# A macaron layer on one core: three stages put into one program block, attention's opening work placed beside the first feed-forward stage and its closing turn split around the opening of the second

## The chip, the cores and the metric

The kernel runs on one core of one Trainium2 chip. The number reported is device time in microseconds (us). The run of the kernel before has a median of 1843.06 us over three executions (1840.89 to 1844.34). One of them, at 1844.34 us, was also recorded by the hardware profiler; every row of a trace below is of that execution. A core has a matmul engine (PE, TensorE), a vector engine (DVE), an activation engine (ACT), a general engine (POOL, GpSimd) and SP, which here only issues DMAs. Each runs its own instructions in program order and waits for the others on semaphores.

## The reference

x has 32 sequences of 256 tokens of width 128, so 8192 rows. Three sublayers follow each other, each on the layer-normalised result of the one before:

```python
x = x + 0.5 * ffn(layernorm(x))     # mixture of experts
x = x + attention(layernorm(x))     # causal, differential, 16 heads of width 8
x = x + 0.5 * ffn(layernorm(x))     # the same weights as the first

# ffn: 8 experts of width 256, two of them picked by a sigmoid gate for each token
comb = zeros(T, 8); comb[top2] = top2_scores / (sum + 1e-6)
h    = silu(einsum('td,ehd->teh', xf, w1))
out  = einsum('te,ted->td', comb, einsum('teh,edh->ted', h, w2))

# attention: two softmaxes over rotated queries and keys, subtracted
attn = softmax(q1 k1) - lam[head] * softmax(q2 k2)
out  = rmsnorm(attn @ v) * head_norm_w * (1 - LAMBDA_INIT);  out @ Wo.T + bo
```

## The kernel before, in words

`build` calls `ffn` (ffn1), `attention`, `ffn` (ffn2). Each of the three opens an `nc.Block()` of its own with one program per engine. Where one block ends and the next begins, all engines meet, and SP first waits until its stores have landed (`sp.wait_ge(stored, ...)`).

**A feed-forward stage** works on 16 blocks of 512 tokens. `blocks` calls `body(Block(c))` on every engine for c = -2 to 16. In the body of block c, PE makes the products of block c, while block c+2 is loaded, normalised and transposed ("read") and block c+1 goes through its gate ("gated"). Inside a body there are eight steps e, one for each expert: PE makes the up product of expert e (L567) into one of two PSUM buffers and the down product of expert e-3 (L580); ACT applies silu (L334) and rounds h to its high part (L341); DVE scales by the gate (`scale`, L479); the low part is made by POOL for experts 0 to 5 (L292) and by DVE for 6 and 7 (L487). The up product of expert e+2 waits for `scale` of expert e, because it writes the same PSUM buffer. The gate runs as: logits on PE (L547), two small DVE operations (L402, L405), two `pow` instructions on POOL (`gate_exp`, L284), thirteen short rounds on DVE that end in `comb` (L470), a transposition (L557), a copy to rows (L328). In the bodies c = -2 and -1 nothing overlaps with products, so there this chain runs bare: the first up product stands in PE's order behind the logits of block 1, and these wait for the rows of block 0. In body -1 POOL runs `gate_exp(0)`, `ln_rstd(1)`, `gate_exp(1)` (the halves of block 0's gate with the reciprocal root of block 1 between them), and DVE runs `mean_shift`, then the gate rounds, with `weight_low(2)` (L499, the low part of w2) in the middle of them at e = 4.

**Attention** works on 32 sequences. `turns` calls `body(Turn(i))` for i = -1 to 34. A turn walks through `ORDER`, a list written by hand of units such as XT (transposition of the normalised x), QK and V (projections), S (scores by query, read by DVE for row maxima), T (scores by key, read by ACT as exp), NT, OT and OP (the end of a sequence); `offset` says which sequence each unit serves in a turn, and `AFTER` says behind which unit the other engines' work stands. Ahead of the turns stands a set-up: SP loads x of sequence 0 and thirteen tensors in all, POOL makes masks, clears `qs` (L997) and `v` (L1000, L1002) and then raises `v_set`; DVE takes statistics of sequence 0, clears `kd` (L1204), makes the low part of the weights (L1211), `biased` in two passes (L1215, L1221) and waits for `v_set` before its first turn. ACT splits `wqk`, then waits for all nine small loads, splits `wv` (L1097), and only then copies the first transposition (L1040). PE's first projection waits for DVE's `xt_low` (L1190). The last turn, 34, holds only the end of sequence 31: ms (DVE L1182, L1185), `rms` (POOL `pow`, L978), `scaled` (POOL L983 to L993), OT, the ACT copy (L1064), OP, the addition (DVE L1178) and the store.

## Time and profile before

| | us |
|---|---|
| median of three runs | 1843.06 |
| the profiled execution | 1844.34 |
| its span, first to last instruction | 1842.6 |
| ffn1: opening, to the first up product | 0 to 32.2 |
| ffn1: products, to the last addition | 32.2 to 433.3 |
| between the last addition and attention's first projection | 433.3 to 450.6 |
| attention's turns, to the last `ms_eps` | 450.6 to 1394.9 |
| from there to ffn2's first up product | 1394.9 to 1439.0 |
| ffn2: products, to the end | 1439.0 to 1842.6 |

PE is busy for 1615.4 us, 88% of the span; DVE 73%, POOL 72%, ACT 65%. By stage PE is busy for 395.8 of 401.1 us in ffn1's products and 395.4 of 403.6 in ffn2's, for 754.3 of 854.9 in attention from 540 to 1394.9, and for 0.7 of 17.3, and 8.6 of 44.1, in the two stretches between the stages. A row of the timeline reads: start, duration, engine, line, operation, tile written <- tiles read, shape, count, and in square brackets how long the engine sat idle before it and what ended that. SPq rows are DMA issues.

### The profile page before, as it was taken

Reading aid. Unit: us, or ns where it says so; the run is one execution under the profiler, and the core shown is the slowest. Engines: PE = TensorE matmul, PEld = TensorE weight load, DVE = VectorE, ACT = ScalarE, POOL = GpSimd, SP = SyncE. Lnnn points to the kernel's source line nnn. Section 1 sums busy time; section 2 is a strip of 40 time slices with the busy share of each in tenths; the row PEclk is TensorE's granted clock in tenths of the full one; section 3 lists DMA queues with packets and bytes.
Section 4 is the critical chain, followed back from the end, with each engine's and each line's share of the span. In section 5 each row is a group of like instructions: output and inputs, shape, how many; then the busy total and the mean of one; then the engine's idle time right before and its main releaser. Section 6 shows DMA issues by size and latency. Waiting matters only on the chain. (4 is left out here: it accounts for less than half of the span.)

```text
span 1842.6 us, 43587 instructions
## 1 busy us (share of the span) xinstructions
PE 1615.4 (88%) x16768; PEld 1235.1 (67%) x16768; DVE 1343.6 (73%) x3034; ACT 1199.4 (65%) x1581; POOL 1319.9 (72%) x836
## 2 busy tenths in 40 slices
PE   4999999995478998988989888998872799999998
PEld 3787778784356666666666666666651688778787
DVE  5777777765678788888878788788732677777775
ACT  4777777772156676666666576676662577777776
POOL 4888888875447677767767677677634688888885
PEclk9999999997589999999999999999996899999999
DMA  3333233332222332332232322332302233233331
GB/s 115 104 116 111 86 104 116 104 104 53 78 67 74 94 89 63 93 92 71 83 88 69 88 83 70 92 87 65 88 17 71 99 115 114 82 105 115 104 110 63
DMA packets 143678, 163.16 MB, mean 89 GB/s; under 512 B 13244, under 2 KB 125582, under 8 KB 142478
## 3 DMA queue, kind: packets, MB, share of 16 engines
q1 hardware_dynamic: 143472, 160.38, 28.5%
q8 instruction: 133, 2.18, 0.5%
q14 instruction: 73, 0.60, 0.1%
HBM read 91.20 MB, written 14.70 MB: 57 GB/s over the span
## 5 line engine op out<-in xcount | busy, mean ns | idle before, releaser
L292 POOL TENSOR_TENSOR ffn_h_low<-ffn_h,ffn_h_high 128x1024 fp32r<-128x1024 f32 x192 | 458.8, 2403 | 94.8 <-ACT ffn_h_high L341 94.8
L1046 ACT ACTIVATE att_prob<-att_ring 128x1024 f32<-128x1024 f32 x384 | 390.3, 1024 | 181.4 <-PE att_ring L1280 180.7
L1159 DVE TENSOR_REDUCE att_nmax<-att_ring 128x4 f32<-128x1024 f32 (+1 forms) x384 | 453.2, 1215 | 39.8 <-PE att_ring L1280 36.8
L479 DVE TENSOR_TENSOR ffn_h<-ffn_up,ffn_comb_wide 128x1024 f32<-128x1024 f32 x256 | 311.1, 1215 | 125.9 <-ACT ffn_up L334 125.7
L334 ACT ACTIVATE ffn_up<-ffn_up 128x1024 f32<-128x1024 f32 x256 | 258.1, 1008 | 201.9 <-PE ffn_up L567 200.2
L341 ACT ACTIVATE ffn_h_high<-ffn_h 128x1024 fp32r<-128x1024 f32 x256 | 269.3, 1052 | 0.7 <-DVE ffn_h L479 0.7
L978 POOL TENSOR_TENSOR att_rrms<-att_ms_eps,att_minus_halves 128x32 f32<-128x32 f32 x32 | 174.1, 5440 | 67.6 <-DVE att_ms_eps L1185 67.6
L1280 PE MATMUL att_ring<-att_qs,att_kd 64*128 64x256 bf16 (+1 forms) x2048 | 153.2, 249 | 76.9 <-DVE att_nmax L1159 24.9
L567 PE MATMUL ffn_up<-ffn_xt_high,ffn_w_high 128*128 128x512 f32 x512 | 214.8, 419 | 1.6 <-DVE ffn_h L479 1.5
L284 POOL TENSOR_TENSOR ffn_ez<-ffn_e_const,ffn_nz 128x16 f32<-128x16 f32 x64 | 185.7, 2903 | 38.8 <-DVE ffn_nz L405 38.8
L580 PE MATMUL ffn_y<-ffn_h_high,ffn_w_high 128*128 128x512 f32 x512 | 205.4, 401 | 6.4 <-POOL ffn_h_low L292 5.0
L1295 PE MATMUL att_o_ps<-att_prob,att_v 128*32 128x256 f32 (+1 forms) x4096 | 201.5, 339 | 5.5 <-ACT att_prob L1046 5.5
L567 PE MATMUL ffn_up<-ffn_xt_low,ffn_w_high 128*128 128x512 f32 x512 | 203.6, 398 | 0.0
L567 PE MATMUL ffn_up<-ffn_xt_high,ffn_w_low 128*128 128x512 f32 x512 | 203.4, 397 | 0.0
L580 PE MATMUL ffn_y<-ffn_h_low,ffn_w_high 128*128 128x512 f32 x512 | 201.4, 393 | 0.0
L580 PE MATMUL ffn_y<-ffn_h_high,ffn_w_low 128*128 128x512 f32 x512 | 200.0, 391 | 0.0
L1280 PE MATMUL att_ring<-att_kd,att_qs 64*128 64x256 bf16 (+1 forms) x2048 | 153.3, 249 | 37.5 <-DVE att_nmax L1159 21.7
L1295 PEld LDWEIGHTS att_o_ps<-att_prob,att_v 128*32 128x32 f32 x4096 | 118.0, 113 | 70.0 <-issue 11.8
L1280 PEld LDWEIGHTS att_ring<-att_qs,att_kd 64*128 64x128 bf16 x2048 | 63.0, 95 | 135.6 <-DVE att_nmax L1159 61.1
L960 POOL TENSOR_TENSOR att_parts<-att_left,att_parts 128x512 bf16<-128x512 f32 x64 | 74.2, 1159 | 100.7 <-ACT att_parts L1057 100.7
L1280 PEld LDWEIGHTS att_ring<-att_kd,att_qs 64*128 64x128 bf16 x2048 | 69.9, 95 | 86.5 <-DVE att_nmax L1159 43.4
L580 PEld LDWEIGHTS ffn_y<-ffn_h_high,ffn_w_high 128*128 128x128 f32 x512 | 96.0, 188 | 42.4 <-POOL ffn_h_low L292 19.2
(152 smaller groups left out, 3248.8 us busy)
## 6 DMA issues: line engine op xcount, KB each, us to landing
ffn_comb_wide<-ffn_comb_d SPq DMA_DIRECT2D x128, 512.0 KB, 5.7
att_qs<-att_parts SPq DMA_DIRECT2D x192, 128.0 KB, 2.4
att_kd<-att_parts SPq DMA_DIRECT2D x192, 128.0 KB, 2.4
ffn_x<-x SPq DMA_DIRECT2D x32, 256.0 KB, 3.1
ffn_w<-w SPq DMA_DIRECT2D x4, 1024.0 KB, 7.6
x<-ffn_out SPq DMA_DIRECT2D x16, 256.0 KB, 2.4
att_x<-x SPq DMA_DIRECT2D x32, 128.0 KB, 2.3
att_xr<-x SPq DMA_DIRECT2D x32, 128.0 KB, 2.3
```

Source lines behind the costliest of these rows:

```text
L284: nc.gpsimd.tensor_tensor(ez[:, k].rearrange("p t e -> p (t e)"), e_const[:, 0:n], nz[:, k].rearrange("p t e -> p (t e)"), ALU.pow).then_i ...
L292: nc.gpsimd.tensor_tensor(hts[1][:, e % NH], h[:, e % NH], hts[0][:, e % NH], ALU.subtract).then_inc(low_by_pool, 1)
L334: nc.scalar.activation(up[:, e % NUP], up[:, e % NUP], ACT.Silu).then_inc(silu_ready, 1)
L341: nc.scalar.activation(hts[0][:, e % NH], h[:, e % NH], ACT.Copy).then_inc(high_ready, 1)
L479: nc.vector.tensor_tensor(h[:, e % NH], up[:, e % NUP], comb_wide[:, b.c % NW, e].unsqueeze(1).to_broadcast([P, HE, FT]), ALU.mult).then_i ...
L567: last = nc.tensor.matmul(up[:, e % NUP, k], w1s[a1][:, col:col + P], xts[a2][:, b.slot()], start=(n == 0), stop=(n == 2))
L580: last = nc.tensor.matmul(y[:], w2s[a1][:, col:col + D], hts[a2][:, e % NH, k], start=(e == 0 and k == 0 and n == 0), stop=(e == E - 1 and ...
L978: nc.gpsimd.tensor_tensor(rrms[:], ms_eps[:], minus_halves[:], ALU.pow).then_inc(rrms_ready, 1)
L1046: nc.scalar.activation(prob[:, u % NP], ring[:, ORDER.index((kind, u)) % 3], ACT.Exp, scale=SCALE).then_inc(prob_ready, 1)
L1159: nc.vector.tensor_reduce(nmax[:, b, :, h0:h0 + cnt], ring[:, pos % 3] .rearrange("p (s h k) -> p s h k", s=2, k=width), AX.X, ALU.max, ne ...
L1280: return nc.tensor.matmul(out, lhs, rhs, start=start, stop=stop)
L1295: last = nc.tensor.matmul(o_ps[VW * i:VW * (i + 1), g % 2, j, b * P:S], v[:, k, b, h], p, start=(b == 0), stop=(b == 1), tile_position=(0, ...
```

## The change

One function, `layer`, replaces `attention` and opens a single block for all three stages. `ffn` no longer runs anything: it returns for each engine a triple of set-up, body and end. The engines' programs are strung together without a meeting point; the joints are waits on counters that exist already. `finished` waits for ffn1's last addition. `gone` (six waits on each engine) is what ffn2's set-up waits for, `banks_free` stands ahead of ffn2's first up product. Tiles of attention that are needed early (`front`) lie where ffn1's raw weights lay, which is why `split_done` stands ahead of their loads; ffn2's tiles lie over attention's except those of the closing turn (`tail`).

Beside ffn1's blocks run now: POOL's masks (ahead of body -1), DVE's `ones_set` (ahead of body 0), SP's mask DMAs (ahead of body 3), the thirteen loads (ahead of body 12), ACT's `split` and DVE's `early` (ahead of body 14), DVE's `late` and POOL's `ln_rstd` (ahead of body 15), DVE's `mean_shift` (ahead of body 16). `kd`, `qs` and `v` are cleared as before, behind `finished`. In both feed-forward stages, in body -1, `ln_rstd(1)` comes behind both halves of `gate_exp(0)`, `mean_shift` behind the gate's first rounds, and `weight_low(2)` at e = 6, behind the gate. The output tile has two slots in place of four, and three PSUM banks change places. At the end of attention `ORDER` of turn 34 is cut: its first unit (with ms and rms) runs, then ffn2's set-up and body -2, then the rest of the turn, then body -1. The first DMA of that cut turn (xr) goes ahead of ffn2's loads and its store behind body -2. The diff, cut to its core:

```diff
+                if e == 1 and read.exists() and b.c != -1:
+                    ln_rstd(read)
+                if e in (0, 1) and gated.exists():
+                    gate_exp(gated, e)
+                if e == 1 and b.c == -1:
+                    ln_rstd(read)
...
+                if e == 6 and b.c == -1:
+                    weight_low(2)
...
+def blocks_beside(program, **beside):
+
+    setup, body, _ = program
+    setup()
     for c in range(-2, FB + 1):
+        if f"before_{c + 2}" in beside:
+            beside[f"before_{c + 2}"]()
         body(Block(c))
...
+def turns(body, first, following):
+
+    setup, ffn_body, end = following
+    for i in range(first, B + 2):
+        body(Turn(i))
+    body(Turn(B + 2), OPENING)
+    setup()
+    ffn_body(Block(-2))
+    body(Turn(B + 2), CLOSING)
+    for c in range(-1, FB + 1):
+        ffn_body(Block(c))
+    if end:
+        end()
...
+        def gone(engine):
+
+            engine.wait_ge(pv_done, 4 * B)
+            engine.wait_ge(prob_ready, 12 * B)
+            engine.wait_ge(pe["T"], 12 * B)
+            engine.wait_ge(o_copied, 4 * B)
+            engine.wait_ge(max_in, 32 * B)
+            engine.wait_ge(left_step, 4 * B)
...
+                blocks_beside(ffn1_sync(sp), before_5=masks, before_14=loads)
+                sp.wait_ge(ones_out, 16)
+                sp.wait_ge(masks_in, 16 * 4)
+                finished(sp)
+                turns(body, -1, ffn_sync(sp))
...
+                blocks_beside(ffn1_gpsimd(pool), before_1=constants, before_17=lambda: ln_rstd(Turn(-2)))
+                finished(pool)
                 clear_queries(0)
...
+                def split():
+                    split_done(act)
+                    act.wait_ge(wqk_in, 16)
+                    nc.scalar.activation(wqks[0][:], wqk[:], ACT.Copy).then_inc(weight_high, 1)
+                    act.wait_ge(weights_in, 16 * 9)
+                    nc.scalar.activation(wvs[0][:], wv[:], ACT.Copy).then_inc(weight_high, 1)
+
+                blocks_beside(ffn1_scalar(act), before_16=split)
+                normalise(Turn(-2))
+                finished(act)
...
+                def early():
+                    split_done(dve)
+                    ln_stats(first)
+                    dve.wait_ge(rope_in, 32)
+                    for u in range(2):
+                        for c in range(2):
+                            last = nc.vector.tensor_scalar(biased[:, u, c], rope[:, 0], bqk[:, 4 * u + c:4 * u + c + 1], None,
+                                                           ALU.mult)
+                    last.then_inc(bias_step, 1)
+
+                def late():
+                    dve.wait_ge(bias_step, 1)
+                    for u in range(2):
+                        for c in range(2):
+                            last = nc.vector.scalar_tensor_tensor(out=biased[:, u, c], in0=rope[:, 1],
+                                                                  scalar=bqk[:, 4 * u + 2 + c:4 * u + 3 + c], in1=biased[:, u, c],
+                                                                  op0=ALU.mult, op1=ALU.add)
+                    last.then_inc(bias_step, 1)
+                    dve.wait_ge(weight_high, 2)
+                    nc.vector.tensor_tensor(wqks[1][:], wqk[:], wqks[0][:], ALU.subtract).then_inc(weight_low, 1)
+                    nc.vector.tensor_tensor(wvs[1][:], wv[:], wvs[0][:], ALU.subtract).then_inc(weight_low, 1)
+
+                blocks_beside(ffn1_vector(dve), before_2=ones_set, before_16=early, before_17=late,
+                              before_18=lambda: mean_shift(first))
+                finished(dve)
```

(The index in `before_17` counts from body -2, so it stands ahead of body 15.)

## Rows read from the trace of the kernel before

**Rows 1.** DVE's timeline in ffn1's opening.

```profile
20.71 0.20 DVE L443 TENSOR_SCALAR ffn_scratch<-ffn_ez 128x32 f32<-128x32 f32 x1 [2.78 <-POOL ffn_ez L284]
...
25.33 2.28 DVE L499 TENSOR_TENSOR ffn_w_low<-ffn_w,ffn_w_high 128x2048 fp32r<-128x2048 f32 x1
...
28.45 0.19 DVE L470 TENSOR_TENSOR ffn_comb<-ffn_scratch,ffn_rdenom 128x32 f32<-128x32 f32 x1
```

**Rows 2.** POOL's timeline in ffn1's opening.

```profile
16.15 1.58 POOL L277 TENSOR_TENSOR ffn_rstd<-ffn_var_eps,ffn_minus_half 128x4 f32<-128x4 f32 x1
```

**Rows 3.** Timelines of DVE, POOL, ACT and PE between ffn1 and attention.

```profile
432.65 0.69 DVE L494 TENSOR_TENSOR ffn_out<-ffn_turn_ps,ffn_x 128x512 f32<-128x512 f32 x1 [3.25 <-PE ffn_turn_ps L591]
...
442.82 1.80 POOL L997 MEMSET att_qs<- 128x2048 uint32 x1
...
447.27 0.30 POOL L1002 MEMSET att_v<- 128x96 f32 x1
...
447.94 0.31 ACT L1097 ACTIVATE att_wv_high<-att_wv 128x128 fp32r<-128x128 f32 x1 [5.80 <-DMA att_lam_in<-lk]
...
450.62 0.55 PE L1280 MATMUL att_ring<-att_xt_high,att_wqk_high 128*128 128x256 f32 x1 [5.92 <-DVE att_xt_low L1190]
```

**Rows 4.** Timelines of DVE, POOL and PE at the turn from body 14 to 15.

```profile
403.02 1.23 DVE L479 TENSOR_TENSOR ffn_h<-ffn_up,ffn_comb_wide 128x1024 f32<-128x1024 f32 x1 [1.56 <-ACT ffn_up L334]
...
401.25 2.41 POOL L292 TENSOR_TENSOR ffn_h_low<-ffn_h,ffn_h_high 128x1024 fp32r<-128x1024 f32 x1 [0.82 <-ACT ffn_h_high L341]
...
405.94 0.40 PE L567 MATMUL ffn_up<-ffn_xt_high,ffn_w_high 128*128 128x512 f32 x1
```

**Rows 5.** DVE's set-up of attention: low weights and both passes of `biased`.

```profile
442.35 1.59 DVE L1211 TENSOR_TENSOR att_wqk_low<-att_wqk,att_wqk_high 128x1024 fp32r<-128x1024 f32 x1
443.87 4.37 DVE L1215 TENSOR_SCALAR att_biased<-att_rope,att_bqk 128x256 f32<-128x256 f32 x4
448.27 1.67 DVE L1221 SCALAR_TENSOR_TENSOR att_biased<-att_rope,att_bqk,att_biased 128x256 f32<-128x256 f32 x4
```

**Rows 6.** DVE and POOL operations side by side, attention's first turn, then body 14.

```profile
465.73 1.11 DVE L1123 SCALAR_TENSOR_TENSOR att_shift<-att_mean_var,att_rstd 128x2 f32<-128x2 f32 x1 [7.44 <-POOL att_rstd L919]
...
465.67 1.16 POOL L960 TENSOR_TENSOR att_parts<-att_left,att_parts 128x512 bf16<-128x512 f32 x1
...
379.50 5.77 POOL L284 TENSOR_TENSOR ffn_ez<-ffn_e_const,ffn_nz 128x16 f32<-128x16 f32 x2
...
380.95 1.21 DVE L487 TENSOR_TENSOR ffn_h_low<-ffn_h,ffn_h_high 128x1024 fp32r<-128x1024 f32 x1
```

**Rows 7.** PE's timeline at a late landing; its window: length, five engines' busy time, clock, DMA share.

```profile
925.43 0.61 PE L1280 MATMUL att_ring<-att_qs,att_kd 64*128 64x256 bf16 x4 [2.46 <-DMA att_qs<-att_max_rows]
...
925.00:930.00 5.00, 4.57 (x56) 3.02 (x56) 1.50 (x3) 2.43 (x3) 0.89 (x2) 0.50 0.52 145
```

**Rows 8.** Timelines of SP, POOL, ACT and DVE between attention and ffn2.

```profile
1394.96 0.42 SPq L868 DMA_DIRECT2D att_xr<-x  x1
...
1407.32 0.36 SPq L221 DMA_DIRECT2D ffn_x<-x  x1
...
1394.99 5.44 POOL L978 TENSOR_TENSOR att_rrms<-att_ms_eps,att_minus_halves 128x32 f32<-128x32 f32 x1 [1.32 <-DVE att_ms_eps L1185]
...
1402.78 0.38 ACT L1064 ACTIVATE att_of_t<-att_ring 128x256 f32<-128x256 f32 x1 [9.70 <-PE att_ring L1360]
...
1413.64 1.63 ACT L316 ACTIVATE ffn_xn<-ffn_x,ffn_shift,ffn_rstd 128x128 f32<-128x128 f32 x4
...
1418.61 3.71 ACT L309 ACTIVATE ffn_w_high<-ffn_w 128x2048 fp32r<-128x2048 f32 x2 [1.48 <-DMA ffn_w<-w]
...
1404.54 0.42 DVE L1178 TENSOR_TENSOR att_xo<-att_ring,att_xrb 128x256 f32<-128x256 f32 x1 [9.63 <-PE att_ring L1280]
...
1420.11 0.19 DVE L405 SCALAR_TENSOR_TENSOR ffn_nz<-ffn_gate_ps,ffn_z_low 128x32 f32<-128x32 f32 x1
...
1435.26 0.19 DVE L470 TENSOR_TENSOR ffn_comb<-ffn_scratch,ffn_rdenom 128x32 f32<-128x32 f32 x1
```

More of the change, by code:

```diff
@@ L732, in attention @@
[L732 to L741 removed]
+        wo = sb("wo", [P, D], to=tail)
@@ new lines, in layer, with raw_weights @@
+        hide_t = sb("hide_t", [P, 4, TILE], BF16, to=tail)
+        halves = sb("halves", [4, 2, S], BF16, to=tail)
+        one_rows = sb("one_rows", [16, 3 * H * S // 16], BF16, to=tail)
+        minus_half = sb("minus_half", [P, QB], to=tail)
+        def raw_weights(to, name):
+            return [to.enter_context(nc.sbuf_tensor(f"{name}_{n}", [P, E * EH], F32)) for n in ("w1", "w2")]
+        raw1 = raw_weights(raw, tag1)
+        raw.close()
+        wqk = sb("wqk", [P, 2 * NC4, P], to=front)
@@ new lines, in layer @@
+        var_eps = sb("var_eps", [P, QB], to=front)
+        rstd = sb("rstd", [P, QB], to=front)
+        shift = sb("shift", [P, QB], to=front)
+        xn = sb("xn", [P, QB, D], to=front)
+        wqks = [sb(f"wqk_{n}", [P, 2 * NC4, P], F32R, to=front) for n in ("high", "low")]
+        wvs = [sb(f"wv_{n}", [P, D], F32R, to=front) for n in ("high", "low")]
+        biased = sb("biased", [P, 2, 2, S], to=front)
+        stage1, (split_done, finished, rows_stored) = ffn(nc, tag1, x_first, x_in, w, *raw1, first_stage, ctx)
@@ L820, in wait_unit, with banks_free, stored_for @@
             wait(engine, pe[kind], turn.at(offset(kind, n), UNITS[kind], n + 1))
+        rest.close()
+        front.close()
+        def gone(engine):
[5 more added lines that the diff above has]
+            engine.wait_ge(left_step, 4 * B)
+        def banks_free(engine):
+            engine.wait_ge(read["OT"], B)
+            engine.wait_ge(read["OP"], B)
+        def stored_for(engine, b):
+            engine.wait_ge(stored, 16 * min(B, FT // S * (b.c + 1)))
+        after = After(sync=gone, gpsimd=gone, scalar=gone, vector=gone, tensor=gone, up=banks_free, stored=stored_for)
+        stage2, _ = ffn(nc, tag2, x_mid, x_out2, w, *raw_weights(ctx, tag2), ctx, ctx, after)
+        ffn_sync, ffn_gpsimd, ffn_scalar, ffn_vector, ffn_tensor = stage2
         with nc.Block() as block:
@@ L860, in set_rows, with body @@
                                      ).then_inc(rows_in[k], 16)
-                def body(turn):
+                def body(turn, part=WHOLE):
                     if turn.runs(2):
                         load_x(turn)
-                    if turn.runs(-3):
+                    if turn.runs(-3) and part is not CLOSING:
                         wait_apart(sp, read["OP"], turn.at(-4, 1, 1))
@@ L1028, in _, with body @@
                 pool.wait_ge(lam_step, 5)
-                turns(body, 0)
+                turns(body, 0, ffn_gpsimd(pool))
             @block.scalar
             def _(act):
-                def body(turn):
-                    for kind, u in ORDER:
+                def body(turn, part=WHOLE):
+                    for kind, u in ORDER[part]:
                         if kind == "XT" and turn.runs(1):
@@ L1211, in _ @@
-                nc.vector.tensor_tensor(wqks[1][:], wqk[:], wqks[0][:], ALU.subtract).then_inc(weight_low, 1)
-                dve.wait_ge(rope_in, 32)
-                for u in range(2):
-                    for c in range(2):
-                        last = nc.vector.tensor_scalar(biased[:, u, c], rope[:, 0], bqk[:, 4 * u + c:4 * u + c + 1], None,
-                                                       ALU.mult)
-                last.then_inc(bias_step, 1)
-                dve.wait_ge(bias_step, 1)
@@ L1423, in build @@
     x2 = nc.dram_tensor("x2", (T, D), F32).ap()
-    ffn(nc, "ffn1", a["x"], x1, a)
-    attention(nc, "att", x1, x2, a)
-    ffn(nc, "ffn2", x2, out, a)
+    layer(nc, a["x"], "ffn1", x1, "att", x2, "ffn2", out, a)
 def kernel(**inputs):
```

1106 lines of the change are left out of this document (552 added, 554 removed).

## The prediction

> **What bounds the kernel now.** I read the page's shares first and then the engines' busy time by stage (both are in the section on the profile). Inside the products of both feed-forward stages PE is busy for 98 to 99% of the time, so there only what makes PE wait counts. In the 17.3 us between ffn1 and attention it is busy for 0.7, in the 44.1 between the last ms_eps and ffn2's first up product for 8.6. In these stretches, and in ffn1's opening, every engine mostly waits for another, so there I read each engine's timeline row by row and looked for what ended last. Attention itself keeps its order of work; its PE losses there are mostly waits for a DMA's landing, which the change doesn't touch. The sum has four terms.
>
> **Term 1, ffn1's opening: -3.6.** The gate's rounds start on DVE at 20.71, as soon as POOL's second gate_exp half is there [rows 1]. Between the halves POOL made rstd of block 1, 1.58 us [rows 2]. Behind both halves it frees 1.58: the gate starts at 19.1. weight_low(2), 2.28 at 25.33, stands inside the rounds; it now follows comb [rows 1]. mean_shift needs rstd(1), now only ready about 1.0 after the second half (the 1.58 held some waiting), so it ends some 0.2 later than its turn. Comb was done at 28.45 + 0.19 = 28.64; now 28.64 - 1.58 - 2.28 + 0.22 = 25.0. Transposition, comb_rows, logits of block 1 and the first up product follow at an unchanged distance. weight_low(2) runs from 25 to 27.3, ahead of the first up product at 28.6. Ends: -3.0, if mean_shift costs 0.8, and -3.6.
>
> **Term 2, attention's work beside ffn1's blocks: +3.0** (0 to +7). Here the change adds instructions ahead of work that PE waits for. What costs nothing: POOL's constants fall where POOL idles before the first gate input comes, SP's 4 masks and 13 loads stand on a queue with nothing urgent but a block's x (asked for two blocks ahead), DVE's ones_set in an idle gap of body 0, ACT's splits (0.31 for the 128 columns of wv [rows 3], about 1.0 for wqk) in its idle time; if their cover were gone, they would cost their own 1 to 6 us once. DVE is what matters, as up(e+2) waits for scale(e). At the turn to body 15 DVE waits 1.56 and does scale at 403.02; PE starts the up product behind it at 405.94, 1.7 us after scale's end at 404.25 [rows 4]. So a scale may be 1.7 late for nothing. late adds 1.67 (four fused passes), 1.59 (wqk_low) [rows 5] and 0.3 (wv_low): 3.55, starting at 401.5. Unhindered it ends at 405.0, scale is 2.0 late, which is close to free. But DVE operations with two SBUF inputs seem to be held while POOL streams: a 128x2 operation that started at 465.73 took 1.11, until POOL's at 465.67 + 1.16 was over [rows 6]. POOL's h_low of 2.41 starts at 401.25 [rows 4] and lasts to 403.66. Thus the first pass is held to there, and late ends at 403.7 + 1.4 + 1.2 + 0.3 + gaps = 406.9 (the 1.67 and 1.59 hold little waits of their own). Scale ends at 408.1, and up(15,1), which stood at 405.94, starts at 408.1: a stall of 2.2. early's tensor_scalars show 4.37 [rows 5], but they start 442.35 + 1.59 to 448.27, beside POOL's clears from 442.82 on [rows 3]; unheld I take about 1.0 for four, ending 1.0 behind their slot, inside the slack of 1.7: nothing. (All 4.37 unhidden would be 2.7 over the slack, which is in the upper end.) mean_shift ahead of body 16 is held until h_low's end: 2.41 after its start, where scale stood at 403.02 - 401.25 = 1.77 [rows 4], so 0.64 + 0.2 = +0.8 in a body that ends the stage. 2.2 + 0.8 = 3.0. The lower end: no holding.
>
> **Term 3, ffn1 to attention: -11.7** (-10.5 to -13). Before: the last addition ends at 432.65 + 0.69 = 433.34. Then come the meeting of the engines, the loads (ACT waited 5.80 for lam_in and split wv until 448.25), xt_low, and the first projection at 450.62 [rows 3]: 17.3. Also in it: POOL's clears, 442.82 to 447.27 + 0.30 = 447.57, so 4.75 [rows 3]. After: loads, splits, statistics, biased and the normalised x of sequence 0 are ready; only POOL's clears remain behind finished, with kd's on DVE, which is shorter. v_set comes at 433.34 + 0.1 + 4.75 = 438.2. DVE waits for it ahead of its first turn, so xt_low (0.4) and the projection come at 438.9. 450.62 - 438.9 = 11.7. What is late next is POOL, alone. PE idles 5.6 in it; after an idle of only 2.46 its clock was granted at 0.50, 1.2 GHz [rows 7], so I assume that level here as before, and no gain. Were it to stay at 2.4 GHz, -1.3 more. The upper end is set-up work of some 1.2 us (SP's set_rows, ACT's copy) that falls behind v_set.
>
> **Term 4, attention's end and ffn2's opening: -13.5** (-9 to -13.5). The anchor is rrms on POOL, 1394.99 + 5.44 = 1400.43; the closing turn's xr load goes out at 1394.96, and x of block 0 now right behind it, at about 1396 in place of 1407.32 [rows 8]. Behind rrms POOL clears small constants and makes rstd(0): together 2.1 (with rstd at 1.58 [rows 2], 2.5). xn of block 0 starts at 1402.55, not 1413.64; nz, which ended at 1420.11 + 0.19 = 1420.30, ends at 1409.2 [rows 8]: 11.1 earlier. ACT's w_high needs 3.71 and had waited for w [rows 8]; the first weights are asked for 11 earlier too, so it ends near 1410.1. Only then come ACT's of_t, OP, and the addition xo: before, from of_t at 1402.78 to xo's end at 1404.96, 2.2 [rows 8]; now the end is 1412.2. So attention's last store, no longer on the path, hides behind the opening. gate_exp(0) on POOL, both halves, 5.77 as in body 14 [rows 6], ends at 1415.0. DVE, behind xo, has statistics of block 1 (about 1.5) and weight_low(1) (2.28 by [rows 1]), to 1416.1: DVE is now late, by 1. The gate's rounds, from 20.71 to 28.64 less the 2.28 [rows 1], are 5.65, with mean_shift 5.8: comb at 1421.95, not 1435.26 + 0.19 = 1435.45 [rows 8]. -13.5. The lower gain: weights land 4.5 later, because x, xr and w share the queues.
>
> **The sum** is -3.6 + 3.0 - 11.7 - 13.5 = -25.8. The profiled execution, 1844.34 (span 1842.6, 1.7 around it), becomes 1818.5, its span 1816.8; it was 1.28 above the median, so the median becomes 1843.06 - 25.8 = **1817.3**.
>
> **The rivals.** **B, cover is complete**: DVE's two-input operations aren't held by POOL, term 2 is 0, and 1814.3. For it: L487 (two SBUF inputs) at 380.95 took 1.21 beside a POOL pow [rows 6]. Against it: 465.73 in the same group, beside a streaming POOL. **C, pow holds as well**: early's operations stand beside gate_exp of body 14, 379.50 to 385.27 [rows 6]. If any POOL instruction held DVE until it ends, they would finish near 386.5, and the scales behind be 5.5 late, less 1.7: +3.8, 1821.1. The row at 380.95 speaks against it. The Trainium skill (SBUF — State Buffer, section "SBUF: two separate sides") has the pair shared by DVE and GpSimd as an exclusive lock "for the whole instruction", for DVE operations in a two-port mode or with two SBUF inputs; taken literally that is rival C, and the trace agrees for the streaming POOL operations only. **D, boundary 2 is worth less**: w lands late or ACT, which takes w_high ahead of of_t, delays xo and with it DVE's statistics: 4.5 less, 1821.8. For it: w had kept ACT waiting 1.48 even behind the engines' meeting [rows 8]. **E, the joints don't overlap**: the joints' waits end so late that only the meetings go and the openings' new order stays. From xo's end, 1404.96, to x's issue at 1407.32 a meeting cost 2.36 [rows 8]; twice that and twice 3.6 make 11.9: 1831.1. Against it: every counter in gone is of turns before the last. **F, slower**: attention's chain from max_rows to qs gets later, since the counters and tiles now carry over from ffn1. PE waited 2.46 for that DMA at 925.43 and ran 5 us at 1.2 GHz in place of 2.4 [rows 7]: 2.46 + 5 x 0.5 = 5.0 for such a turn. From 6 more such turns on (30 us) the gain is gone; in 28 turns it would be +140 - 26, so 1957. Against it: order, buffers and DMAs within the turns stay the same.
>
> **How the numbers follow.** Forecast 58%, B 12%, C 10%, D 12%, E 4%, F 4%. The range takes in forecast, B, C and D with the ends of the terms: low 1811.5 (term 2 at 0, term 3 at -13, with half of what term 4 may yet give), high 1826.0 (C and D together give 1825.6). E and F stay out. A measurement can tell 0.2%, 3.7 us, about the spread of the three runs. Every case but F is faster by more: faster 0.94; 0.02 for F stopping near six turns; slower 0.04.
>
> **What would show it.** Term 1: DVE's first gate rounds at 19.1, comb near 25.0, first up near 28.6. Term 2: up(15,1) waits about 2.2 for scale, late's first pass starts or ends at POOL's h_low's end, and no wait in bodies 12 to 14; if late's rows show their bare durations, B. Term 3: first projection 5.6 after the last addition, released by xt_low behind v_set, POOL without a gap. Term 4: x of block 0 issued within 2 us of xr, xn about 2 behind rrms, xo between bodies -2 and -1, first up 30.6 after the last ms_eps, where 44.1 stood. The prediction is wrong if attention's turns take longer, if ACT's w_high ends much after 1410 on this scale, or if PE starts ffn2 with a stall at a weight.

## The result: 1843.7 to 1815.85 us

Over four executions each, the median went from 1843.7 us (1840.89 to 1845.09) to 1815.85 (1811.61 to 1820.04), a ratio of 0.985 with a 95% interval of 0.982 to 0.988. That is 27.9 us less; forecast were 25.8 less and 1817.3. The profiled execution took 1812.79, its span is 1811.0, against 1844.34 and 1842.6 before: 31.6 less. Its six stretches (start of the first up product; to the end of the last addition; to the first projection; to the last ms_eps; to ffn2's first up product; to the end) show where they went. A joint is the stretch between two stages; the second is counted from the start of the last ms_eps, 0.2 ahead of its end, from which the 44.1 and 30.6 of the prediction count.

| stretch | before | changed | difference | forecast |
|---|---|---|---|---|
| ffn1, opening | 32.17 | 29.38 | -2.79 | -3.6 |
| ffn1, products | 401.17 | 403.39 | +2.22 | +3.0 |
| first joint | 17.28 | 5.45 | -11.83 | -11.7 |
| attention | 944.11 | 938.17 | -5.94 | 0 |
| second joint and ffn2's opening | 44.25 | 30.96 | -13.29 | -13.5 |
| ffn2, products | 403.62 | 403.65 | +0.03 | 0 |

The four stretches that have a forecast term changed by -25.69 together, where -25.8 stood. The rest of the profiled difference is attention, whose turns the change leaves alone.

In every timeline row below, the columns are start, duration, engine, line, operation, tile written <- tiles read, shape, count, and in brackets the idle time before it and what ended it. First PE at the landmarks of the changed kernel, the first projection among them, which answers to the last row of [rows 3]:

```profile
29.38 0.77 PE L574 MATMUL ffn_up<-ffn_xt_high,ffn_w_high 128*128 128x512 f32 x1
...
404.75 0.50 PE L574 MATMUL ffn_up<-ffn_xt_high,ffn_w_high 128*128 128x512 f32 x1 [1.54 <-DVE ffn_h L485]
...
438.22 0.55 PE L1398 MATMUL att_ring<-att_xt_high,att_wqk_high 128*128 128x256 f32 x1 [4.93 <-DVE att_xt_low L1295]
...
1407.35 0.77 PE L574 MATMUL ffn_up<-ffn_xt_high,ffn_w_high 128*128 128x512 f32 x1
```

**The opening of ffn1**, POOL and then DVE, against [rows 1, 2]:

```profile
13.23 6.33 POOL L282 TENSOR_TENSOR ffn_ez<-ffn_e_const,ffn_nz 128x16 f32<-128x16 f32 x2 [2.03 <-DVE ffn_nz L411]
19.54 1.00 POOL L275 TENSOR_TENSOR ffn_rstd<-ffn_var_eps,ffn_minus_half 128x4 f32<-128x4 f32 x1
```

```profile
14.53 2.28 DVE L505 TENSOR_TENSOR ffn_w_low<-ffn_w,ffn_w_high 128x2048 fp32r<-128x2048 f32 x1
19.68 0.20 DVE L449 TENSOR_SCALAR ffn_scratch<-ffn_ez 128x32 f32<-128x32 f32 x1 [2.86 <-POOL ffn_ez L282]
...
25.64 0.19 DVE L476 TENSOR_TENSOR ffn_comb<-ffn_scratch,ffn_rdenom 128x32 f32<-128x32 f32 x1
```

rstd now takes 1.00 where it took 1.58 in the middle [rows 2]. The 0.58 didn't vanish: the pair of pow instructions takes 6.33, and two such took 5.77 in [rows 6]. POOL was waiting in its second instruction until DVE's weight_low, 14.53 + 2.28 = 16.81, was over, and whichever instruction stands second bears that.

**The price beside the blocks**, DVE and POOL at bodies 15 and 16, against [rows 4]:

```profile
398.48 3.74 DVE L1327 SCALAR_TENSOR_TENSOR att_biased<-att_rope,att_bqk,att_biased 128x256 f32<-128x256 f32 x4
402.14 1.21 DVE L1332 TENSOR_TENSOR att_wqk_low<-att_wqk,att_wqk_high 128x1024 fp32r<-128x1024 f32 x1
...
423.05 2.27 DVE L1228 SCALAR_TENSOR_TENSOR att_shift<-att_mean_var,att_rstd 128x2 f32<-128x2 f32 x1
```

```profile
398.35 2.40 POOL L290 TENSOR_TENSOR ffn_h_low<-ffn_h,ffn_h_high 128x1024 fp32r<-128x1024 f32 x1 [0.82 <-ACT ffn_h_high L344]
...
422.92 2.39 POOL L290 TENSOR_TENSOR ffn_h_low<-ffn_h,ffn_h_high 128x1024 fp32r<-128x1024 f32 x1 [0.36 <-ACT ffn_h_high L344]
```

The first fused pass begins as POOL streams h_low (to 400.75), and the four take 3.74 in place of 1.67 [rows 5]. mean_shift, on 128x2 elements, takes 2.27, to POOL's 425.31.

**The first joint**: POOL's three clears run from 432.83 to 437.56, DVE's xt_low stands right behind them, and nothing else is late:

```profile
432.83 1.81 POOL L1097 MEMSET att_qs<- 128x2048 uint32 x1 [7.53 <-DVE ffn_out L500]
434.57 2.66 POOL L1102 MEMSET att_v<- 128x3072 f32 x1
437.30 0.26 POOL L1104 MEMSET att_v<- 128x96 f32 x1
```

```profile
433.27 1.76 DVE L1340 MEMSET att_kd<- 128x2048 uint32 x1 [0.49 <-DVE ffn_out L500]
437.64 0.43 DVE L1295 TENSOR_TENSOR att_xt_low<-att_ring,att_xt_high 128x256 fp32r<-128x256 f32 x1 [2.61 <-POOL att_v L1104]
```

**The second joint**, SP, POOL, ACT and DVE, against [rows 8]. The last ms_eps starts at 1376.39:

```profile
1377.28 0.36 SPq L212 DMA_DIRECT2D ffn_x<-x  x1
...
1376.65 5.44 POOL L1078 TENSOR_TENSOR att_rrms<-att_ms_eps,att_minus_halves 128x32 f32<-128x32 f32 x1 [1.32 <-DVE att_ms_eps L1290]
...
1382.84 1.02 POOL L275 TENSOR_TENSOR ffn_rstd<-ffn_var_eps,ffn_minus_half 128x4 f32<-128x4 f32 x1
...
1396.59 2.22 POOL L275 TENSOR_TENSOR ffn_rstd<-ffn_var_eps,ffn_minus_half 128x4 f32<-128x4 f32 x1
...
1384.09 1.65 ACT L319 ACTIVATE ffn_xn<-ffn_x,ffn_shift,ffn_rstd 128x128 f32<-128x128 f32 x4 [1.96 <-DVE ffn_shift L396]
...
1388.50 3.71 ACT L312 ACTIVATE ffn_w_high<-ffn_w 128x2048 fp32r<-128x2048 f32 x2 [0.90 <-DMA ffn_w<-w]
1392.12 0.36 ACT L1166 ACTIVATE att_of_t<-att_ring 128x256 f32<-128x256 f32 x1
...
1393.86 0.42 DVE L1283 TENSOR_TENSOR att_xo<-att_ring,att_xrb 128x256 f32<-128x256 f32 x1 [3.08 <-PE att_ring L1398]
...
1395.66 2.28 DVE L505 TENSOR_TENSOR ffn_w_low<-ffn_w,ffn_w_high 128x2048 fp32r<-128x2048 f32 x1
1397.86 0.19 DVE L449 TENSOR_SCALAR ffn_scratch<-ffn_ez 128x32 f32<-128x32 f32 x1
```

x of block 0 is asked for 0.66 behind xr (1376.62), xn starts 2.0 behind rrms. ACT's w_high waited 0.90 for w, of_t stands behind it, xo behind of_t, weight_low(1) behind xo, and the gate's rounds start when that is over, at 1397.86, though both pow instructions were done at 1396.63.

### The profile page after: what moved, and what is told of

The parts are those of the page before. It is cut to its first block, busy times and chain, and to the rows that moved or that the text cites. A ratio compares the mean times of both kernels' runs of the same rounds, so it can differ in the third digit from the quotient of the medians.

```text
span 1811.0 us, 43617 instructions
## 1 busy us (share of the span) xinstructions
PE 1607.8 (89%) x16768; PEld 1229.6 (68%) x16768; DVE 1345.2 (74%) x3034; ACT 1198.5 (66%) x1581; POOL 1320.1 (73%) x836
## 3 DMA queue, kind: packets, MB, share of 16 engines
q1 hardware_dynamic: 143472, 160.38, 28.9%
## 4 chain that ended last, share of the span: by engine, by line
PE 44%; POOL 22%; issue 13%; DVE 11%; DMA 4%; ACT 4%; SPq 2%; POOLq 0%; DVEq 0%; ACTq 0%
PE att_ring L1398 13%; PE ffn_y L587 9%; PE ffn_up L574 9%; POOL ffn_ez L282 8%; PE att_o_ps L1413 7%; DVE att_nmax L1264 6%; POOL ffn_h_low L290 5%; POOL att_rrms L1078 3%; PE att_ring L1473 2%; POOL ffn_rstd L275 2%; DMA att_max_rows<-att_nmax_t 2%; ACT att_prob L1148 2%; ACT ffn_h_high L344 2%; DMA att_qs<-att_max_rows 2%; DVE att_turned L1243 1%
```

## Experiments

Executions of one kernel differ by several us, most of it in attention, so the experiments are read by the six stretches of their profiles, which repeat to within 0.1 to 0.5 where nothing was changed; the second joint adds to that up to 1.3, with w late by 0 to 1.2 on ACT, and attention varies by ten. Medians stand beside them. All edits are to the changed kernel.

| kernel | ffn1 opening | ffn1 products | joint 1 | attention | joint 2 | ffn2 | median |
|---|---|---|---|---|---|---|---|
| changed | 29.38 | 403.39 | 5.45 | 938.17 | 30.96 | 403.65 | 1815.85 |
| e1_order_undone | 32.29 | 403.53 | 5.45 | 944.17 | 35.57 | 403.79 | 1827.55 |
| e2_no_cover | 29.37 | 401.31 | 17.00 | 937.91 | 29.97 | 403.84 | 1821.81 |
| e3_turn_whole | 29.59 | 403.60 | 5.45 | 945.22 | 39.39 | 404.05 | 1831.66 |
| e4_v_wait_later | 29.56 | 403.45 | 2.68 | 937.83 | 30.00 | 403.78 | 1819.62 |
| e5_late_beside_pow | 29.43 | 405.81 | 5.45 | 939.02 | 29.95 | 403.84 | one run |
| e6_spread | 29.35 | 402.99 | 5.45 | 940.23 | 29.95 | 403.73 | one run |
| e7_low1_earlier | 30.94 | 403.63 | 5.45 | 938.09 | 31.73 | 403.86 | one run |
| e8_one_block_only | 29.41 | 401.24 | 15.60 | 948.48 | 31.28 | 403.69 | one run |
| e9_changed_again | 29.41 | 403.72 | 5.44 | 941.55 | 30.90 | 403.78 | 1820.0 |
| e10_best | 29.39 | 402.86 | 1.70 | 942.99 | 30.65 | 404.11 | 1817.07 |

e1 to e4 ran on one chip, beside 1846.83 for the kernel before; e9 and e10 on a second, beside 1848.86. e5 to e8 ran once each on a third (1815.23, 1813.44, 1815.47 and 1831.41, beside a single 1837.36), so they are read by their stretches alone.

### The order of body -1

```diff
-                if e == 1 and read.exists() and b.c != -1:
+                if e == 1 and read.exists():
                     ln_rstd(read)
                 if e in (0, 1) and gated.exists():
                     gate_exp(gated, e)
-                if e == 1 and b.c == -1:
-                    ln_rstd(read)
...
-                if e == 2 and read.exists() and b.c != -1:
+                if e == 2 and read.exists():
                     mean_shift(read)
...
-                if e == 2 and b.c == -1:
-                    mean_shift(read)
-                if e == 6 and b.c == -1:
+                if e == 4 and b.c == -1:
                     weight_low(2)
```

> The changed kernel, with body -1 of both feed-forward stages in the old order (rstd of block 1 between the two halves of the gate's exponential, mean_shift ahead of the gate's rounds, weight_low(2) inside them). Landmarks of the changed kernel's profile: first up product at 29.4 us, ffn1's products until the last addition 403.4, from there to the first projection 5.45, from the first projection to the last ms_eps 938.2, from there to ffn2's first up product 31.0, ffn2's products 403.6. My theory (the order counts in both openings, as DVE's gate rounds are the last chain in each): first up product at 32.2 (+2.8), and 33.9 in place of 31.0 at the second joint, +5.7 in all. Rival 1 (at the second joint DVE is late anyway because of the closing turn, so the order is worth nothing there): +2.8 in all. Rival 2 (the order counts for nothing, and ffn1's opening got shorter for another reason, such as an earlier landing): 0. All other stretches unchanged, except attention's, which may move by 6 either way.

The first opening got 2.9 longer, as expected. The second went to 35.57, and the kernels in which w landed in time show 29.95 to 30.00 there. Here w was in time too, so it got 5.6 longer, not 2.9. POOL and DVE of this kernel say why:

```profile
1399.90 2.91 POOL L282 TENSOR_TENSOR ffn_ez<-ffn_e_const,ffn_nz 128x16 f32<-128x16 f32 x1 [4.91 <-DVE ffn_nz L409]
1403.87 2.98 POOL L275 TENSOR_TENSOR ffn_rstd<-ffn_var_eps,ffn_minus_half 128x4 f32<-128x4 f32 x1 [1.06 <-DVE ffn_var_eps L388]
1406.83 2.89 POOL L282 TENSOR_TENSOR ffn_ez<-ffn_e_const,ffn_nz 128x16 f32<-128x16 f32 x1
```

```profile
1401.90 0.42 DVE L1279 TENSOR_TENSOR att_xo<-att_ring,att_xrb 128x256 f32<-128x256 f32 x1 [2.08 <-PE att_ring L1394]
...
1403.71 2.28 DVE L503 TENSOR_TENSOR ffn_w_low<-ffn_w,ffn_w_high 128x2048 fp32r<-128x2048 f32 x1
```

With the closing turn's addition ahead of it on DVE, var_eps of block 1 comes late, and rstd, standing between the two pow instructions, first waits 1.06 for it and then is held by weight_low until 1405.99. So the order and the split of the turn belong together: the split alone would have brought POOL a new wait in the middle of the gate.

### The overlap with ffn1's blocks

```diff
-                blocks_beside(ffn1_sync(sp), before_5=masks, before_14=loads)
+                blocks_beside(ffn1_sync(sp), before_5=masks)
+                loads()
...
-                blocks_beside(ffn1_gpsimd(pool), before_1=constants, before_17=lambda: ln_rstd(Turn(-2)))
+                blocks_beside(ffn1_gpsimd(pool), before_1=constants)
+                ln_rstd(Turn(-2))
...
-                blocks_beside(ffn1_scalar(act), before_16=split)
+                blocks_beside(ffn1_scalar(act))
+                split()
...
-                blocks_beside(ffn1_vector(dve), before_2=ones_set, before_16=early, before_17=late,
-                              before_18=lambda: mean_shift(first))
+                blocks_beside(ffn1_vector(dve), before_2=ones_set)
+                early()
+                late()
+                mean_shift(first)
```

> The changed kernel, with attention's thirteen loads, the splits, statistics, biased, rstd and mean_shift moved from beside ffn1's blocks to behind ffn1's last body; one block and no meeting of the engines, as in the changed kernel. My theory (it is the overlap that shortens the first joint, and the price beside the blocks is real): ffn1's products 401.2 in place of 403.4, and 14 (12.5 to 15.5) from the last addition to the first projection in place of 5.45, since the loads take some 9 to land and DVE's biased then meets POOL's clears again. Net +6.4. Rival 1 (the meeting of the engines was what cost): joint below 8, net about 0. Rival 2 (the meeting cost nothing): joint 17.3 as before the change, net +9.7.

ffn1's products fell to 401.31: the work beside the blocks costs 2.1. The joint took 17.00, not 14, near the 17.3 of rival 2 (the meeting cost nothing). But this order of the work is not that of the kernel before; the chain is another. Rows of DVE and ACT:

```profile
436.58 4.57 DVE L1322 TENSOR_SCALAR att_biased<-att_rope,att_bqk 128x256 f32<-128x256 f32 x4 [1.57 <-DMA att_bqk<-bqk]
```

```profile
442.94 0.31 ACT L1202 ACTIVATE att_wv_high<-att_wv 128x128 fp32r<-128x128 f32 x1 [6.13 <-DMA att_lam_in<-lk]
444.82 0.88 ACT L1187 ACTIVATE att_xn<-att_x,att_shift,att_rstd 128x128 f32<-128x128 f32 x2 [1.57 <-DVE att_shift L1231]
```

In this order mean_shift and xn stand behind everything of late, which the old order did not have, and late waits for the last small load. My 14 had left that out. So this run shows what the overlap covers in this order (11.5), not what the meeting cost. For that, the opening work went behind ffn1 in its old order, the constants and masks too:

```diff
-                blocks_beside(ffn1_sync(sp), before_5=masks, before_14=loads)
+                blocks_beside(ffn1_sync(sp))
+                loads()
+                masks()
...
-                blocks_beside(ffn1_vector(dve), before_2=ones_set, before_16=early, before_17=late,
-                              before_18=lambda: mean_shift(first))
+                blocks_beside(ffn1_vector(dve))
                 finished(dve)
+                ones_set()
+                ln_stats(first)
+                mean_shift(first)
```

> The changed kernel, with all of attention's opening work (constants, masks, loads, splits, statistics, biased, low parts) behind ffn1's last body, in the order in which the kernel before had it, so that at the first joint only the meeting of the engines and SP's final wait for its store are gone. In the kernel before SP issued the first load 2.8 after the last addition; here right behind the last store, some 0.6 after it. My theory (the meeting cost what it delayed the first load): 15.1 from the last addition to the first projection, in place of 17.3 before and 5.45 in the changed kernel, and ffn1's products 401.2. Rival 1 (the meeting cost nothing): 17.3. Rival 2 (it hid more, as engines could run ahead into their set-up): below 12.

15.60, by one execution, where 15.1 was expected: the meeting and SP's final wait were worth 1.7 of the 11.8 at this joint, the overlap the other 10.1, against 2.1 to 2.2 paid in the blocks.

### The split of the closing turn

```diff
-    body(Turn(B + 2), OPENING)
+    body(Turn(B + 2))
     setup()
     ffn_body(Block(-2))
-    body(Turn(B + 2), CLOSING)
```

> The changed kernel, with attention's last turn run as a whole ahead of ffn2's set-up and body -2. My theory (x of block 0 is then asked for behind the last store, 10 us later than 1377.3, and the opening hangs on it): ffn2's first up product 39.5 (38 to 41) behind the last ms_eps in place of 31.0, +8.5. Rival 1 (rrms on POOL, 5.4 us, sets the end, and what stands behind it in either order costs only its own 4.5): +4.5. Rival 2 (the split is worth nothing, w's landing sets the end): 0.

39.39, where 39.5 was expected. SP's queue shows what the opening hung on:

```profile
1394.23 0.36 SPq L992 DMA_DIRECT2D x<-att_xo  x1
1394.83 0.36 SPq L212 DMA_DIRECT2D ffn_x<-x  x1
```

The last ms_eps starts at 1383.86 there, so x is asked for 11.0 behind it, against 0.9 in the changed kernel. The split is worth 8.4 against the changed kernel's profile (9.4 against those with w in time). No run takes the second meeting out alone, but its price can be read: from xo's end, x is asked for 2.36 behind it in the kernel before (1404.96 to 1407.32, [rows 8]) and 0.74 behind it here (1394.09 to 1394.83). That is 1.6, and with the order at the first opening's 2.9 and the split's 8.4 it makes up nearly all of the 13.29.

### What holds a DVE operation beside POOL

```diff
-                blocks_beside(ffn1_vector(dve), before_2=ones_set, before_16=early, before_17=late,
+                blocks_beside(ffn1_vector(dve), before_2=ones_set, before_16=lambda: (early(), late()),
```

> The changed kernel, with DVE's late (four fused passes, wqk_low, wv_low) put directly behind early, ahead of body 14 in place of body 15. There POOL runs gate_exp's two pow instructions and not h_low. In the changed kernel the four passes took 3.74 us, until POOL's h_low ended, and the up product behind waited 1.54. My theory (a DVE operation with two SBUF inputs is held while POOL streams, and not while POOL computes a pow): the four passes take 1.2 to 1.7, wqk_low 1.2; in body 14 the scale behind them starts 3.1 later, of which 0.8 is slack, so PE waits about 2.3 there, and not at all in body 15; ffn1's products 404.1 in place of 403.4. Rival 1 (these passes are slow on their own): 3.7 here too, PE waits 4.5 in body 14, products 406.3. Rival 2 (any POOL instruction holds them until it ends, pow too): they end only with the second pow, near 382.8 on the changed kernel's scale, the scale behind is 6.6 late, PE waits 5.8.

DVE and POOL of this kernel:

```profile
378.21 1.68 DVE L1327 SCALAR_TENSOR_TENSOR att_biased<-att_rope,att_bqk,att_biased 128x256 f32<-128x256 f32 x4
```

```profile
377.01 6.97 POOL L282 TENSOR_TENSOR ffn_ez<-ffn_e_const,ffn_nz 128x16 f32<-128x16 f32 x2
```

The four passes take 1.68 beside pow and 3.74 beside h_low: rivals B and C of the prediction both fall, B since the holding is real, C since a pow that computes doesn't hold. PE waited 2.0 in body 14, near the 2.3 expected, and not in body 15. What I had wrong is the sum: 405.81, not 404.1. The difference is PE's clock. In these rows of PE a product takes 0.50 right behind the wait and 0.63 two us later:

```profile
382.41 0.50 PE L574 MATMUL ffn_up<-ffn_xt_high,ffn_w_high 128*128 128x512 f32 x1 [2.00 <-DVE ffn_h L485]
...
384.27 0.63 PE L587 MATMUL ffn_y<-ffn_h_high,ffn_w_high 128*128 128x512 f32 x1
```

From 384.4 to 386.8 the granted clock is 0.50, 1.2 GHz. The 24 products from 382.41 on take 7.23 us; behind the changed kernel's wait of 1.54 (at 404.75), where the clock stays at 1.00, 24 take 5.66. So the 0.46 more of waiting brought 1.57 of lost clock with it, which is nearly all of the 1.7 that I had missed.

The pow pair itself grew, from 5.77 in [rows 6] and 6.19 at the same place of the changed kernel to 6.97: its second instruction, which began beside wqk_low, took 4.10 in place of 2.90. The holding goes both ways, but here PE waited for none of it.

Of the other way, e7 was meant as an improvement and became the measurement:

```diff
-                if e == 0 and b.c == -1:
-                    weight_low(1)
...
                 if e == 7 and read.exists():
                     logits(read)
+                if e == 7 and b.c == -2:
+                    weight_low(1)
```

> The changed kernel, with DVE's weight_low(1) (2.28) at the end of body -2 in place of the start of body -1, in both feed-forward stages. In the changed kernel DVE stood idle for 3.1 before the closing turn's addition, and weight_low(1) behind it ended 1.2 after the gate's exponential was ready. My theory (DVE is the late one at the second joint, by that 1.2): from the last ms_eps to ffn2's first up product 28.8 to 29.8 in place of 31.0; in ffn1's opening POOL's second pow is no longer held by it, first up product at 28.9 in place of 29.4. Rival (ACT's copies, or w's landing, are the late ones): both unchanged, or later by up to 2.3 where weight_low waits for ACT ahead of the addition.

Both openings got longer, 1.5 and 1.8 (against 30.0), where both were expected to get shorter. The rival's number (later by up to 2.3) fits, but neither of its reasons is in the trace: w was in time, and the closing turn's addition came no later. DVE and POOL of the first opening are:

```profile
13.20 2.28 DVE L505 TENSOR_TENSOR ffn_w_low<-ffn_w,ffn_w_high 128x2048 fp32r<-128x2048 f32 x1
```

```profile
13.36 7.76 POOL L282 TENSOR_TENSOR ffn_ez<-ffn_e_const,ffn_nz 128x16 f32<-128x16 f32 x2 [2.03 <-DVE ffn_nz L411]
```

The pow pair takes 7.76, 1.99 more than 5.77. weight_low began 0.16 ahead of it and ended at 15.48, 2.12 after its start. The first pow took 4.89 and the second 2.90, as if the first began to work only then. A pow that has begun isn't disturbed: in the changed kernel weight_low ran from 14.53, within the first pow, which took 2.92, and only the second paid (3.45).

The third try was to pay less for the same work:

```diff
-                blocks_beside(ffn1_vector(dve), before_2=ones_set, before_16=early, before_17=late,
+                blocks_beside(ffn1_vector(dve), before_2=ones_set, before_15=early, before_16=late, before_17=lows,
```

(`lows` is the second half of `late`: wqk_low and wv_low; loads and splits move one body earlier.)

> The changed kernel, with the same instructions beside ffn1's blocks spread over three bodies: loads ahead of body 11, statistics, tensor_scalars and ACT's splits ahead of body 13, the four fused passes ahead of body 14, wqk_low and wv_low ahead of body 15, mean_shift where it was. My theory (a scale may be about 1 late for nothing in each body, so the same work costs less in smaller portions): the wait of the up product in body 15 falls from 1.54 to 0.3, nothing new elsewhere, ffn1's products 402.2 in place of 403.4. Rival (each portion is held by POOL's h_low at the start of its body and pays again): 403.4 or more.

The wait for scale in body 15 is gone, but body 13 has one of 0.28, and PE waited 0.71 there for POOL's low part, where the changed kernel shows 0.15. The products took 402.99, 0.4 less than in the changed kernel's first profile and 0.7 less than in its second (e9), where 1.2 less was expected. Each portion is held again: the four passes took 3.42 ahead of body 14, and wqk_low took 3.35 ahead of body 15, in place of 1.21.

### What is left at the first joint

```diff
                             wait(dve, pv_done, turn.at(1 - NSLOT, 4, 4))
+                            if turn.c == -1:
+                                dve.wait_ge(v_set, 1)
...
-                dve.wait_ge(v_set, 1)
                 body(first.after())
```

> The changed kernel, with one line moved: DVE waits for POOL's clearing of v not ahead of its first turn but ahead of its first write into v. My theory (POOL's clears are the only thing that holds the first projection, and POOL is free again before it has to rotate): first projection 1.6 to 2.0 behind the last addition in place of 5.45, first rotation on POOL 3.5 earlier, -3.5 in all; up to 1.3 more if PE's clock is still high. Rival (POOL is the limiter of the first turn whatever the projection does): the projection moves, POOL's first rotation stays at 9.8 behind the last addition, 0 in all.

The joint fell to 2.68, not to 1.8: DVE's clearing of kd stands ahead of xt_low and became the next limit, in these rows of DVE.

```profile
433.50 1.76 DVE L1342 MEMSET att_kd<- 128x2048 uint32 x1 [0.49 <-DVE ffn_out L500]
435.18 0.36 DVE L1297 TENSOR_TENSOR att_xt_low<-att_ring,att_xt_high 128x256 fp32r<-128x256 f32 x1
```

The gain wasn't given back, as the rival had it: POOL's first rotation came 7.0 behind the last addition in place of 9.75, and from the projection to POOL's first rms took 102.85, against 103.30 and 103.09 in the two profiles of the changed kernel. The last version moves that clearing behind xt_low too, and takes the spread order:

```diff
                             nc.vector.tensor_tensor(xts[1][:], ring[:, pos % 3, 0:S], xts[0][:],
                                                     ALU.subtract).then_inc(xt_low, 1)
+                            if turn.c == -1:
+                                clear_keys(0)
...
-                clear_keys(0)
                 dve.wait_ge(weights_in, 16 * 9)
-                dve.wait_ge(v_set, 1)
                 body(first.after())
```

> The changed kernel with three edits: DVE waits for v's clearing only ahead of its first write into v, DVE clears kd behind its first xt_low, and the work beside ffn1's blocks is spread over bodies 13, 14 and 15. My theory: first joint 1.5 in place of 5.45 (the transposition 0.1, ACT's copy, xt_low, each straight behind the other), up to 1.3 more in the first projection if PE's clock stays high; ffn1's products 403.0; the sum 4.4 faster than the changed kernel in these stretches. Rival 1 (POOL's clears, over 4.8 behind the last addition, or SP's rows, are the next limit of the first turn): the projection moves and the first rotation on POOL stays at 7 behind the last addition, so 1 faster than the run with the first edit alone gained, at most. Rival 2 (the rows of kd are now set too late for the first scores): PE's wait for them grows from 6.2 by what was gained.

The joint is 1.70, the products 402.86; PE and POOL:

```profile
433.95 0.35 PE L1402 MATMUL att_ring<-att_xt_high,att_wqk_high 128*128 128x256 f32 x1 [1.18 <-DVE att_xt_low L1297]
```

```profile
437.46 1.28 POOL L1051 TENSOR_TENSOR att_qk<-att_turned 128x512 f32<-128x512 f32 x1 [0.41 <-DVE att_turned L1243]
```

The first projection takes 0.35, not 0.55 as at 438.22, so PE's clock was still high after an idle of 1.18. It did not stay so: from 434.99 on a projection takes 0.41 again, and the 24 up to V's first took 4.43 in place of 4.55. The 1.3 that a lasting clock was to bring, here and in term 3 of the prediction, did not come; it was 0.1. POOL's first rotation follows 5.2 behind the last addition's end (432.25), against 9.75 in the changed kernel, and PE's longest wait for the rows of kd is 6.1, where 6.2 stood: neither rival. The three stretches up to the first projection are 4.6 shorter than those of e9, and the median of six executions is 1817.07 against 1820.0 of five of the changed kernel on the same chip; the intervals of the two ratios to before (0.981 to 0.987, and 0.983 to 0.987) overlap, so the whole time alone doesn't prove it, the stretches do.

### Attention's 6 us

> The changed kernel itself, unaltered, beside the version below and the kernel before. Its six stretches in the profiles so far: first up product 29.4, ffn1's products 403.4, first joint 5.45, attention 938.2, second joint 31.0, ffn2's products 403.7. My theory (the 6 that attention gave in its first profile are no effect of the change, but chance: the same stretch measured 937.8 to 948.5 in eight kernels that leave the turns alone, and all of it lies in turns with a late landing of max_rows): all stretches but attention's within 0.3 of these, the second joint 30.0 where w lands early enough, attention anywhere from 937 to 949. Rival (the change made attention's turns shorter by 6): 937 to 939 again.

All stretches but attention's came back within 0.33. Attention took 941.55. Over the eleven profiles of the changed kernel and its variants, none of which touches the regular turns, it takes 937.8 to 948.5, and the 944.11 before lies inside that range, above eight of the eleven. So the first profile's 938.17 shows no effect of the change. With one profile of the kernel before, a small effect isn't excluded either. A regular turn takes 26.84 before and after; turns with a late max_rows take longer. PE's waits in attention, before and changed (in us: total, times, longest):

```profile
PE att_ring L1280 <- DMA att_qs<-att_max_rows: 20.2, 13, 2.6
```

```profile
PE att_ring L1398 <- DMA att_qs<-att_max_rows: 19.9, 13, 2.1
```

Number and sum are the same, the longest isn't. What that is worth is seen in the same turn (from rms to rms) of both, by windows: stretch, length, busy time of PE, PEld, DVE, ACT and POOL, granted clock, DMA share, GB/s. Before, then changed:

```profile
909.20:940.50 31.30, 27.23 (x416) 19.43 (x412) 21.96 (x34) 18.33 (x26) 19.70 (x17) 0.89 0.26 73
```

```profile
895.20:923.40 28.20, 24.45 (x416) 18.02 (x412) 22.75 (x34) 18.22 (x26) 19.70 (x17) 1.00 0.29 81
```

The same 416 matmul rows; after a wait of 2.46 [rows 7] PE worked part of the turn at 1.2 GHz, after one of 1.9 it did not, and 3.1 us lie between them. Two such turns (this one, and 31.3 against 28.4 four turns later) make up the 6 of the profile. The length of the wait alone doesn't decide it: in e4 a wait of 2.39 left the granted clock at 1.00 and the turn took 28.66, while in e8, after a wait of 1.98, the clock was granted at 0.70 over the next 11 us and the turn took 30.78. Nothing in these runs ties such turns to the change.

## Why the prediction was right, step by step

**Term 1** (-3.6, was -2.79). The order was right; moving rstd was over-valued. I freed the whole 1.58 of [rows 2] though I had noted that it held some waiting; 0.58 of it was the wait for weight_low, and it passed to the second pow. The gate started at 19.68, not 19.1. weight_low(2) was over-valued too: without its 2.28 the round behind it still starts 0.26 after the one ahead (24.46 to 24.72), where 2.27 stood before, so 2.01 came free. The two make up the 0.8.

**Term 2** (+3.0, was +2.22). The mechanism is as forecast, row by row: holding until h_low's end, passes and low parts behind it until 403.56, PE's wait 1.54 where 2.2 stood. The size was off by small waits that I had left in the durations of [rows 5]: late ended 5.2 behind h_low's start, not 5.65. One price is missing from the term, and that it didn't fall due is luck: it takes a stall of 2.2 at full clock. Behind 1.54 the clock did stay; behind 2.00, in e5, it fell and cost 1.57 more. Ahead of body 16, mean_shift made PE wait 0.62 for DVE's low part, where 0.8 stood. By e2 and e8, which have none of this work beside the blocks, the whole is 2.1 to 2.2.

**Term 3** (-11.7, was -11.83). The chain named, POOL's clears at 4.75, took 4.73. PE ran the first projections at 1.2 GHz, as assumed.

**Term 4** (-13.5, was -13.29). Each point came within half a us: xn 2.0 behind rrms, xo between bodies -2 and -1, DVE late by 1.2, which is why w's 0.9 of lateness went through to the end. What the prediction didn't see is how the two edits hang together: rival E puts the order at the same 3.6 in both openings, and with the split in place it is worth 5.6 in the second.

**The rivals.** B and C are refuted by e5, one execution, by the length of the four passes. D's mechanism, w late and DVE behind xo, is real, at 0.96 and not 4.5: the changed kernel and e9 show 30.9, those with w in time 30.0. E: the meeting alone is worth 1.7 at the first joint and, by the issue of x, 1.6 at the second, less than the 2.36 assumed. F: the turns' base is unchanged. The range's low end takes 1.5 more from term 4 than that term's own range (-9 to -13.5) allows; nothing hung on it.

**The total** was right by the terms (-25.69), and the 2.2 between them and the median's 27.9 stand in no term; attention's spread from profile to profile is larger than that. In e9's session the same two kernels stand at 1820.0 and 1848.86, 28.9 apart.

The rule of the Trainium skill (SBUF — State Buffer, section "SBUF: two separate sides") that DVE and GpSimd exclude each other on a shared pair agrees with the trace in that either makes the other wait: 3.74 in place of 1.68, and 7.76 in place of 5.77. "For the whole instruction" doesn't fit POOL's pow, beside which the four passes ran at 1.68.

## What to carry to other kernels

Cost an operation that is laid beside another engine's work by what that engine is doing at that moment, not by its own duration: the same four passes were 1.7 beside a pow and 3.7 beside a streaming subtraction, and a 128x2 operation took 2.3. When an instruction with a wait inside is moved out of a chain, the wait stays with whoever is next. Ask of every stall how PE's clock comes out of it: 0.46 us more of waiting came with 1.57 of slower products. And measure parts together as well as apart: an order worth 2.9 in the first opening was worth 5.6 in the second, behind the other edit. Read them in stretches of the trace when the whole varies by more than the part.

## What the runs showed of the hardware that was not expected

A POOL pow on 16 elements a partition (2.9 us) neither held DVE's passes nor was held once it ran, but its start was: with DVE's 2.28 us subtraction begun 0.16 before it, the pair of pow took 7.76 in place of 5.77; with it begun 1.3 into the first pow, 6.33. A plain tensor_scalar on DVE is held by POOL's streaming too: var_eps of attention (128x2) took 1.08 beside h_low, in place of 0.17 with POOL idle (e2), and four tensor_scalars took 4.57 beside POOL's clears, and 1.18 beside pow.

The late landings of max_rows have a pattern. By the DMA view of each turn, before and changed, seven turns, four or five apart, move four packets on the queue of instructions (q8) in place of three, and in each of them max_rows takes 2.5 to 3.7 us to land in place of 1.5; five more turns are late without that. That fetching instructions delays the landing is not tested here.
